# A graph network on one core: three gathered bodies over four pairs of counted groups, and VectorE adds the three parts of the sums

## The reference, cut to what matters

```python
src_h = h[src] @ W_msg.T + b_msg
emb = edge_embed[jnp.clip(edge_type, 0, NUM_EDGE_TYPES)]
messages = jax.ops.segment_sum(src_h + emb, dst, num_segments=num_nodes)
h_new = _gru_cell(messages, h, W_ih, W_hh, b_ih, b_hh)
...
x = _layernorm(x + _L0_gnn_ref(x, edge_index, edge_type_9, ...), axis=-1)
x = _layernorm(x + _L1_gnn_ref(x, fc_weight, attn, eps, src, dst), axis=-1)
```

## Time and profile before

| | us |
|---|---|
| median of 3 runs | 3324.41 |
| the profiled execution | 3325.84 |
| its span | 3324.0 |
| TensorE's matmuls busy | 2133.7 (64%) |
| VectorE busy | 2487.7 (75%) |
| GpSimd busy | 2221.1 (67%) |
| ScalarE busy | 1562.8 (47%) |

### The profile page before, as it was taken

The page is one execution under the profiler, slowest core; times in us unless marked ns, Lnnn a source line. Parts: engine busy times, 40 slices in busy tenths (PEclk is TensorE's granted clock), DMA queues, the critical chain, the costliest instruction groups (busy, mean ns, idle before and its releaser), DMA issues. The chain is left out here.

```text
span 3324.0 us, 64226 instructions
## 1 busy us (share of the span) xinstructions
PE 2133.7 (64%) x13619; PEld 1702.8 (51%) x13619; DVE 2487.7 (75%) x12615; ACT 1562.8 (47%) x3370; POOL 2221.1 (67%) x2275
## 2 busy tenths in 40 slices
PE   1398988999899845555555555655555555555553
PEld 1266666666674444444445554544554545444442
DVE  6566666666654578888887887888888888888888
ACT  2255544455553345445454454454454454545541
POOL 2467777777730037777777777777777777777772
PEclk9999999999999877677676667666666666766665
DMA  7222222222220085555555555555555555555562
GB/s 138 79 68 76 74 74 74 76 76 75 77 79 1 23 235 156 169 163 157 169 160 161 168 158 165 164 157 167 165 156 169 163 159 168 159 164 164 158 168 66
DMA packets 364818, 431.96 MB, mean 130 GB/s; under 512 B 178859, under 2 KB 247845, under 8 KB 364788
## 3 DMA queue, kind: packets, MB, share of 16 engines
q0 software_dynamic: 107760, 274.39, 29.0%
q1 hardware_dynamic: 254815, 156.62, 17.7%
q10 hardware_dynamic: 2212, 0.60, 0.1%
HBM read 407.68 MB, written 23.70 MB: 130 GB/s over the span
## 5 line engine op out<-in xcount | busy, mean ns | idle before, releaser
L1385 POOL DMA_INDIRECT got<-rows,idx x1624 | 1548.1, 953 | 536.0 <-issue 510.1
L1551 PE MATMUL sum_ps<-whot,got 128*128 128x128 f32 x3264 | 680.4, 377 | 663.2 <-DVE whot L1397 590.7
L1551 PEld LDWEIGHTS sum_ps<-whot,got 128*128 128x128 f32 x3264 | 585.4, 269 | 750.6 <-DVE whot L1397 658.5
L727 POOL DMA_INDIRECT got<-x_rows,idx x616 | 625.0, 1015 | 196.6 <-issue 187.4
L1544 PE MATMUL er_ps<-win,hot_t 128*128 128x128 bf16 x4932 | 524.5, 284 | 254.7 <-ACT hot_t L1495 230.5
L870 ACT CAST work<-c_ps 128x318 bf16<-128x318 f32 x1008 | 420.0, 428 | 482.4 <-PE c_ps L943 473.8
L1453 DVE CUSTOM_DVE_ANT_0 pr_s<-got,er_ps 128x128 f32<-128x128 f32 x1624 | 370.2, 284 | 363.8 <-DMA got<-rows,idx 357.9
L1544 PEld LDWEIGHTS er_ps<-win,hot_t 128*128 128x128 bf16 x4932 | 464.9, 133 | 297.0 <-ACT hot_t L1495 260.0
L894 PE MATMUL span_ps<-x_parts,work 128*126 128x393 bf16 x2544 | 583.9, 339 | 0.0
L1397 DVE TENSOR_SCALAR whot<-iota_f,dl,w_s 128x128 f32<-128x128 f32 x1632 | 459.1, 359 | 0.3 <-ACT w_s L1500 0.3
L1525 ACT ACTIVATE r_s<-er_ps 128x512 f32<-128x512 f32 x406 | 242.4, 597 | 381.3 <-DVE er_ps L1465 379.1
(11 more groups left out here) (238 smaller groups left out, 1823.5 us busy)
## 6 DMA issues: line engine op xcount, KB each, us to landing
work<-dst_row SPq DMA_DIRECT2D x413, 256.0 KB, 3.7
got<-rows,idx POOLq DMA_INDIRECT x1624
win<-parts SPq DMA_DIRECT2D x118, 96.0 KB
got<-x_rows,idx POOLq DMA_INDIRECT x616
idx<-src_rows SPq DMA_DIRECT2D x413, 2.0 KB
parts<-split SPq DMA_DIRECT2D x13, 384.0 KB, 3.3
x_rows<-x_parts SPq DMA_DIRECT2D x1, 4641.0 KB
rows<-nodes SPq DMA_DIRECT2D x13, 256.0 KB, 3.5
```

The source lines that it names most:

```text
L727: pool.indirect_dma_start(got[:, c, i, 0:3 * D], None, x_rows, bass.IndirectOffsetOnAxis(ap=idx[:, c, i:i + 1], axis=0)).then_inc(gathered ...
L1385: pool.indirect_dma_start(got[:, c, i, :], None, rows, bass.IndirectOffsetOnAxis(ap=idx1[:, c, i:i + 1], axis=0)).then_inc(gathered[c], 16)
L1551: mm = pe.matmul(sum_ps[:, 0:P], got[:, c, i, D:2 * D], whot[:, c, i, :], start=(c == 0 and i == 0), stop=(c == NS - 1 and i == STEP - 1))
```

## The change

`GATHERED` goes from 22 to 19: 84 tiles (three bodies) are now counted, four groups more. There are 26 pairs and 19 bodies. The loop over pairs becomes a loop over six *rounds* of four pairs (`ROUND`), with three bodies (`PER_ROUND`) spread over the round's 168 steps: 56 steps (`SPACE`) for each. 18 bodies lie so beside pairs 1 to 24; pair 25 has none, and the 19th body comes last.

The three parts of a sum are now added on VectorE: `fold` and `fold_last` (two float32 additions of 126 by 128 and a cast of the nine kinds to bf16) before `post`, which has one float32 product and one bf16 product for the kinds, at step 13 in place of 5. `fold_body` and `fold_body_last` do the same for a body. VectorE also makes a second, bf16 `place_b`.

```diff
-GATHERED = 22
+GATHERED = 19
+ROUND = 4
+PER_ROUND = 3
...
-            POST, BLOCKS = 5, 2
-
-            TILE_AT = {5 + 36 * n // GROUP: n for n in range(GROUP)}
-            HOT_AT = {1 + 10 * c: c for c in range(NC)}
-            POST_AT, ADD_AT = 2, 2 * CG - RING
+            POST, BLOCKS = 13, 2
+            FOLD = 8
+
+            ROUNDS = BESIDE // PER_ROUND
+            SPACE = 2 * CG * ROUND // PER_ROUND
+            TILE_AT = {SPACE * u + 5 + (SPACE - 6) * n // GROUP: (u, n) for u in range(PER_ROUND) for n in range(GROUP)}
+            HOT_AT = {SPACE * u + 1 + SPACE // NC * c: (u, c) for u in range(PER_ROUND) for c in range(NC)}
+            BEGIN_AT = {SPACE * u: u for u in range(PER_ROUND)}
+            POST_AT = {SPACE * u + 16: u - 1 for u in range(PER_ROUND)}
+            FOLD_AT = {SPACE * u + 6: u - 1 for u in range(PER_ROUND)}
+            ADD_AT = {SPACE * u + SPACE // 2: u - 1 for u in range(PER_ROUND)}
+            DRAIN_AT = {SPACE * u + SPACE - 1: u for u in range(PER_ROUND)}
...
+                        dve.tensor_scalar(place_b[0:ROWS, h, :], iota_f[0:ROWS, :],
+                                          column_no[0:ROWS, :, :].rearrange("p b g -> p (b g)")[:, bass.ds(g, 1)],
+                                          None, ALU.is_equal).then_inc(place_done, 1)
+
+                    def fold(g, h):
+
+                        dve.wait_ge(s_copied, g + 3)
+                        dve.wait_ge(posted, g + 1)
+                        dve.tensor_tensor(whole_s[0:ROWS, h, :], turned_s[0:ROWS, h, 2 * D:3 * D],
+                                          turned_s[0:ROWS, h, D:2 * D], ALU.add).then_inc(half_folded, 1)
+                        dve.tensor_copy(kinds_b[0:ROWS, h, :], turned_s[0:ROWS, h, 3 * D:PW]).then_inc(folded, 1)
+
+                    def fold_last(g, h):
+                        dve.wait_ge(half_folded, g + 1)
+                        dve.tensor_tensor(whole_s[0:ROWS, h, :], whole_s[0:ROWS, h, :],
+                                          turned_s[0:ROWS, h, 0:D], ALU.add).then_inc(folded, 1)
+
+                    def fold_body(j):
+                        dve.wait_ge(drained, j + 2)
+                        dve.wait_ge(body_posted, j + 2)
+                        dve.tensor_tensor(whole_body[:], body_s[:, 2 * D:3 * D], body_s[:, D:2 * D], ALU.add
+                                          ).then_inc(body_half, 1)
...
                     def post(g, h):
-                        pe.wait_ge(s_copied, g + 3)
-                        pe.wait_ge(place_done, g + 1)
+                        pe.wait_ge(folded, 2 * g + 2)
+                        pe.wait_ge(place_done, 2 * g + 2)
                         pe.wait_ge(added, 2 * g + 2)
-                        for i in range(3):
-                            pe.matmul(out_ps[:, 0:P], turned_s[0:ROWS, h, i * D:(i + 1) * D], place[0:ROWS, h, :],
-                                      start=(i == 0), stop=(i == 2))
-                        pe.matmul(out_ps[0:NT, P:2 * P], turned_s[0:ROWS, h, 3 * D:PW], place[0:ROWS, h, :],
+                        pe.matmul(out_ps[:, 0:P], whole_s[0:ROWS, h, :], place[0:ROWS, h, :], start=True, stop=True)
+                        pe.matmul(out_ps[0:NT, P:2 * P], kinds_b[0:ROWS, h, :], place_b[0:ROWS, h, :],
                                   start=True, stop=True).then_inc(posted, 1)
...
+                                if t == FOLD and not first:
+                                    fold(g - 2, h)
+                                if t == FOLD + 1 and not first:
+                                    fold_last(g - 2, h)
...
-                    with dve.Fori(1, BESIDE + 1) as k:
-                        make_pair(k, False, True)
-                    with dve.Fori(BESIDE + 1, PAIRS) as k:
-                        make_pair(k, False, False)
+                    with dve.Fori(0, ROUNDS) as r:
+                        for p in range(ROUND):
+                            make_pair(ROUND * r + p + 1, False, p, r)
+                    with dve.Fori(ROUNDS * ROUND + 1, PAIRS) as k:
+                        make_pair(k, False)
```

More of the change, by code:

```diff
@@ L621, in graph_layers @@
             place = sb("place", [P, 2, P], F32, ph)
+            place_b = sb("place_b", [P, 2, P], BF16, ph)
+            whole_s = sb("whole_s", [P, 2, D], F32, ph)
+            kinds_b = sb("kinds_b", [P, 2, NT], BF16, ph)
+            whole_body = sb("whole_body", [P, D], F32, ph)
             c_ps = psum("c_ps", [P, CB, 512], F32, ph)
@@ L789, in _, with make_pair @@
                     dve.reg_mov(last_at, 0)
-                    def make_pair(k, first, beside):
+                    def make_pair(k, first, p=None, r=None):
                         for h in range(2):
@@ L860, in drain, with copy_pair @@
                         act.copy(body_s[:], sum_ps[:, 0:PW]).then_inc(drained, 1)
-                    def copy_pair(k, first, beside):
+                    def copy_pair(k, first, p=None, r=None):
                         for h in range(2):
@@ L927, in post_body, with count_pair @@
                         pe.wait_ge(body_added, 2 * j + 4)
-                        for i in range(3):
-                            pe.matmul(body_ps[:, 0:P], body_s[:, i * D:(i + 1) * D], ident[:],
-                                      start=(i == 0), stop=(i == 2))
+                        pe.wait_ge(body_folded, j + 2)
+                        pe.matmul(body_ps[:, 0:P], whole_body[:], ident[:], start=True, stop=True)
                         pe.matmul(body_ps[0:NT, P:2 * P], body_s[:, 3 * D:PW], ident[:],
                                   start=True, stop=True).then_inc(body_posted, 1)
-                    def count_pair(k, first, beside):
+                    def count_pair(k, first, p=None, r=None):
                         steps = CG - BLOCKS
@@ L950, in count_pair @@
                                     post(g - 2, h)
-                                if beside and CG * h + t == POST_AT:
-                                    post_body(k - 2)
-                                if beside and CG * h + t in TILE_AT:
-                                    sum_tile(k - 1, TILE_AT[CG * h + t])
+                                at_round = None if p is None else 2 * CG * p + CG * h + t
+                                if at_round in POST_AT:
+                                    post_body(PER_ROUND * r + POST_AT[at_round])
+                                if at_round in TILE_AT:
+                                    u, i = TILE_AT[at_round]
+                                    sum_tile(PER_ROUND * r + u, i)
                     pe.sem_inc(posted, 2)
@@ L958, in _ @@
                     pe.sem_inc(body_posted, 1)
-                    count_pair(0, True, False)
+                    count_pair(0, True)
                     pe.wait_ge(zeroed0, 3)
-                    with pe.Fori(1, BESIDE + 1) as k:
-                        count_pair(k, False, True)
-                    with pe.Fori(BESIDE + 1, PAIRS) as k:
-                        count_pair(k, False, False)
+                    with pe.Fori(0, ROUNDS) as r:
+                        for p in range(ROUND):
+                            count_pair(ROUND * r + p + 1, False, p, r)
+                    with pe.Fori(ROUNDS * ROUND + 1, PAIRS) as k:
+                        count_pair(k, False)
                     ready(CGN - 1)
```

63 lines of the change are left out of this document (46 added, 17 removed).

## The result

| | us |
|---|---|
| changed kernel, median of 6 | 3309.48 (3307.39 to 3312.14) |
| before, median of 6 | 3322.98 (3315.03 to 3326.8) |
| ratio | 0.9959, 95% interval 0.9945 to 0.9973 |
| profiled execution, its span | 3310.75, 3308.9 |

13.5 us are gained where 78 were forecast; 3309 lies outside the range of 3210 to 3290. In three sets of runs (the first four, four that were repeated, and two with loops of seven and three pairs in the kernel before) every kernel, the one before too, took 4230 to 4410 us, with waits between engines of up to 46 us, for a cause that the traces don't name; these are called the *long sets*, and of them the stalls inside one engine are used and no small ratio.

The account below looks back on a forecast made before the run. GpSimd's gathers were taken to bound the kernel; afterwards a closed chain of 40.0 us a body would. The loop saves 80.7 us, preparation and tail add 2: 3325.8 to 3247, 3246 at the median's level, range 3210 to 3290.

Parts of the forecast that it names:

- A rule against it: VectorE's five jumps back: instruction fetch might stall 2.4 us each, 12 us if unhidden; VectorE's lead hides it, costed at nothing.
- The tie: Chain from gathers through TensorE, VectorE's chunk 3 one-hots and SyncE to the next body's gathers: 40.0 us a body.
- TensorE's work: Products beside a body: 28.6 us a pair, 38.1 for a body's 56 steps; `post` falls from 1.08 to 0.33.
- VectorE's additions at nothing: Folds, casts and `place_b` on VectorE: 24.4 of 30 us a pair, 1.4 lost waiting for ScalarE's copy; costed at nothing.
- Preparation and tail: Before and after the loop over pairs: ninth block of counted tiles and more dependent additions, +1 us each.
- TensorE alone as the pace: Rival in the loop over pairs: TensorE's 38.1 us a body sets the time, giving 3214; chance 0.2.
- The longer tie: Rival in the chain between bodies: low clock after waits and VectorE late, 42.6 us a body, 3290; chance 0.2.
- Lockstep of VectorE and TensorE: Rival in the groups: VectorE late at the fold idles TensorE once a group, 37.0 us a pair, 3415; chance 0.06.
- That GpSimd bounds it anyhow: Rival in the gathers: 532 gathers each 0.15 us slower beside VectorE's extra work cancel the 80 us gain; chance 0.04.
- the groups of pair 25: Sign in the last pair, which has no body beside it: groups take 12.3 us.
- GpSimd's wait for indices once a body: Sign between bodies: GpSimd, gapless before, waits for `idx` about 3 us once a body.
- No wait of the count (`c_ps`) for VectorE's `right` of over a microsecond: Sign in TensorE's count products: they never wait over a microsecond for VectorE's tile.

Follow-up runs that it names:

- the best kernel: Loops over rounds written out and one-hots of chunks 1 to 3 made earlier (both edits), against the changed kernel: 3226.25 us, 0.971 of before.
- one half: The spreading of bodies without VectorE's additions, `post` back at step 5, loops kept, against the changed kernel: 3275.84 us, 0.9832 of before.

## Why the prediction was wrong, step by step

The loop came to 786.3 + 24.3 us; the forecast had 718.1 + 24.6. The miss of 68.2 in pairs 1 to 24 has two terms.

**"A rule against it": 43.6 us, the step that failed.** The prediction wrote that VectorE is "one to two batches (4 to 9 us) ahead of TensorE there, so I give it nothing". The kernel with loops written out takes 43.6 us less in pairs 1 to 24, 8.7 a jump. Three things were wrong. VectorE stands for 6.2 us and not 2.4, a small DMA's time: the nearest row was of another kind of fetch. VectorE's lead was 3.8 us: it ends the round with `add_group`, which waits for `post`, and the change had put `post` at step 13 of 21 (the 5.97 us wait at 541.88), after which only one batch is left. The forecast counted the later `post` for the group's sums and not for VectorE's lead. And TensorE's own jump was left out: its branch lasts 3.7 to 4.3 us, of which the products queued before it cover 1.9. In the changed kernel VectorE's stall ends last and so sets the time. Of the 8.7 us a jump 5.1 are waits; the other 3.6 go with the stretch at 1.2 GHz behind them. By the kernel without additions, which loses 1.7 us a jump to TensorE's branch alone, some 7 of the 8.7 are VectorE's; that is an estimate, since only runs of a long set write out one engine's loop alone.

The Trainium skill (Runtime: NRT & Kernel Launch, Instruction fetch mechanics) has it that a taken branch out of the current window of two pages, each of 256 instructions, stalls for a fetch. The trace agrees for VectorE's loops of 591 (4.1 us a jump) and 640 (6.2 us) instructions and for TensorE's of 1,818 (3.7 to 4.3 us in the branch). VectorE's loop of 461 is shorter than two pages and stalls as well (3.75 to 4.29 us); it could lie over three pages, which no run here shows.

**The tie: 24.6 us, right in kind, too short by 1.4 a body.** Without jumps a body takes 742.7 / 18 = 41.3 us, where the forecast had 718.1 / 18 = 39.9. The links, as means over bodies 1 to 17 of the version written out: the 21 gathers of chunks 0 to 2 take 28.4 (27.7 forecast); from there to TensorE's first product of chunk 2, 2.3 (1.8); to the end of chunk 3's one-hots, 5.1 (5.7); to SyncE's first load, 0.24 (0.3); to the next first gather, 5.1 (4.5). Sum 41.2, forecast 40.0. So the gathers, the landing and SyncE's loads were each 0.5 to 0.7 short and VectorE's part 0.6 long. The changed kernel's body at 452.25 is one of its longer ones, with TensorE's wait at 483.66 and the loads here:

```profile
490.18 0.34 SPq L712 DMA_DIRECT2D dst_now<-dst_left  x1
```

In it the 21 gathers take 481.87 - 452.25 = 29.6, because a few gathers are long.

```profile
454.75 1.91 POOL L745 DMA_INDIRECT got<-x_rows,idx  x1 [0.30 <-issue]
...
478.98 2.89 POOL L745 DMA_INDIRECT got<-x_rows,idx  x1 [0.30 <-issue]
```

VectorE's timeline has a body's wide one-hots beside the second:

```profile
478.55 1.07 DVE L814 TENSOR_TENSOR hot<-iota_f,dl 128x896 bf16<-128x896 f32 x1
```

That the link exists and is what binds is shown by moving the one-hots: it gave 56.2 us with jumps kept, 42.1 without.

**TensorE's work: right.** 38.1 a body was forecast; the best kernel takes 38.9, of which its waits for gathers are 0.7 (13.1 us in 18 bodies). The kinds' product took 0.16 and not 0.08, and a `post` 0.47, not 0.33:

```profile
590.94 0.39 PE L977 MATMUL out_ps<-place,whole_s 126*128 126x128 f32 x2
591.25 0.22 PE L978 MATMUL out_ps<-place_b,kinds_b 126*9 126x128 bf16 x1
591.41 0.31 PE L1010 MATMUL c_ps<-right,left 128*128 128x318 bf16 x1
```

So 0.62 is saved a group, 0.75 forecast.

**VectorE's additions at nothing: right inside a round, wrong at its end.** The waits for ScalarE's copy are 22.7 us in 40, 0.6 each where 1.4 was foreseen, and TensorE doesn't wait for VectorE but at jumps. But the products that they save bring nothing while the tie sets the pace: by the runs they cost 10 us, together with `post` at step 13, with the one-hots where the change has them (3268 against 3258, written out), and give some 18 only once the tie is gone.

**Preparation and tail**, +2 in the forecast, were -0.7 and -1.6.

**The rivals.** TensorE alone as the pace: no, except in the version with both edits. The longer tie (42.6 a body): closest in time, 43.7, but for another reason, since the tie itself is 41.3 and the rest are jumps. Lockstep of VectorE and TensorE: not in a round; at its end TensorE does wait for VectorE, once in eight groups, but for a jump and not for the fold. That GpSimd bounds it anyhow: no, it idles 120 us; its gathers did get slower, by 0.027 us each (1042 ns against 1015) of the 0.15 that this rival needs. **What was to show it**: the groups of pair 25 (12.45) and GpSimd's wait for indices once a body (6 us and not 3) did; "No wait of the count (`c_ps`) for VectorE's `right` of over a microsecond" is the sign that failed. TensorE's clock over 0.95 came true (0.96) and told nothing, since it was 0.96 before.

*Left open*: where between 169 and 461 instructions VectorE's stall begins, and between 503 and 1,818 TensorE's; what each engine's jump is worth by itself; and what a later or earlier `post` does without the additions. None was tried.

## What to carry to other kernels

When a change multiplies the instructions of a loop, price each jump back, on every engine that has the loop, with the stall measured here (some 6 us from the branch to VectorE's next operation, 3.3 to 4.3 us in TensorE's branch) against that engine's lead *at the jump*, and read the lead from the last wait before it. When a view names a releaser, look whether it had long been done: TensorE's own jump stood here under VectorE's name. When an engine that waits in a closed chain is relieved, relieve the chain's latest link first (here one column of a table, worth more than the whole change). And run the halves of a change apart: here one half was worth four times the whole.

## What was not expected of the hardware

- Loops of 461 to 1,073 recorded instructions stall VectorE at each jump back: its queue stands for 2.7 to 3.3 us and again for 2.1 to 2.8, and the engine idles for 3.75 to 6.5, by how far the queue was ahead. Loops of 155 and 169 don't.
- TensorE's loop of 1,818 recorded instructions holds its queue for 3.3 to 4.3 us in the branch; one of 503 for 0.2. ScalarE's of 371 isn't held.
- Gathers issued by GpSimd take longer while VectorE makes the wide one-hots (L814, 1.08 us, both inputs in SBUF), here up to three times. Between 150 and 980 us of the changed kernel 62 gathers with VectorE idle beside their first 0.94 us took 0.947 us, none over 0.95; 356 beside its other work 0.976; and 102 beside `hot` 1.34, the longest 2.98.
- A wait of 0.99 us (at 525.19) left the granted clock at 1.00 in the four microseconds behind it, one of 2.05 (at 483.66) was followed by 0.58, and one of 4.06 with another of 1.06 close behind it by 0.50 in 551 to 555.
